# A mixture-of-experts layer on one core: three of four experts in seven products instead of two, casts and y tiles moved to ScalarE

## Chip, core and metric

The kernel runs on one core of a Trainium2 chip. The metric is the device time of one execution in microseconds, lower is better. Before the change the median of three runs is 317.22 us.

## What is computed

```python
x = x + tanh(g_xattn) * attention(layernorm(x), ctx)      # 2 x 1024 tokens of 256, 16 heads of 64, 64 context rows
h = layernorm(x)
probs = softmax(h.mean(axis=1) @ gate_w); top_w, top_i = top_k(probs, 2)     # per batch of 1024 tokens, 8 experts
for e in top_i:                                           # F = 1024
    hmid = gelu(h @ w1[e] + b1[e])
    out += top_w[e] * (hmid @ w2[e] + b2[e])
x = x + tanh(g_ffn) * out
```

Routing is per batch, so two batches need two experts each: four expert passes, numbered 0 to 3.

## The kernel before

**Precision.** Each float32 operand is a pair of float32r tiles: `_hi`, a rounded copy, and `_lo`, the remainder. A product is three matmuls (hi x hi, hi x lo, lo x hi). ScalarE makes most `_hi` tiles, VectorE the `_lo` tiles.

**Stages.** After the setup, a loop over 16 token tiles does attention in steps (scores, softmax, transposes of the probabilities from `sx`, products with `vw`). In it GpSimd multiplies the probabilities by the reciprocal sums (L563) and refines the layernorm factors by Newton steps (`y_rstds`, L529 to L535). The two last steps of the loop also start expert 0 (`EARLY`: hidden blocks 0, 1, 2). Then come the four expert passes, and the residual tiles are stored.

**Plain passes (experts 0 and 1 of the first batch).** For each of two chunks of 512 tokens and eight blocks f of 128 hidden columns, TensorE does `first_layer` (6 matmuls of 512 columns, into bank 4 or 5), ScalarE the Gelu into `gel`, VectorE `split(n)`: a cast to `h_hi` (L1318) and the subtraction to `h_lo` (L1320). TensorE does `second_layer` (6 matmuls) for the block two, in the first chunk four, behind. `first_layer(n)` from block 5 on waits for the Gelu of block n - 2, whose bank it takes. Along expert 0, eight y tiles of the second batch are made: GpSimd subtracts the mean and scales (L594, L597), TensorE transposes (L1658), ScalarE and VectorE make `yT_hi` and `yT_lo`. The next expert's weights are split in 32 pieces.

**Seven-product passes (experts 2 and 3 of the second batch).** A unit g handles blocks f and f + 4 for both chunks. Instead of eight block products of 3 matmuls it does seven, of sums and differences of weights (`wx`, from `block_sum`) and tokens (`t`, from `differences`). In between, TensorE does eight half second layers of the unit before (`behind_unit`, parts 0 to 7). ScalarE copies partial results out of the banks (`snapshot`, L855), VectorE adds (`block_total`, L1403), and four Gelus named C11, C22, C12, C21 read the sums. The order of unit 0 is P1, half, P2, half, P6, half, P5, P7, half, P3, P4; of the others half, P1, half, P2, half, P6, half, P5, half, P7, half, P3, half, P4, half (in unit 1 two halves precede P1). P7 waits for the second snapshot, P4 for the second total, P1 of the next unit for the Gelu C21.

**Order of work.** Each engine's program is written out by hand and runs in order; semaphores join them. A wait holds all that stands behind it on that engine. `FREE_SPLITS` is the constant 4 by which `w2_done` starts ahead, added by TensorE after the attention loop.

Of the kernel before, what the change touches and what calls it, by code (L numbers as in the profile page):

```python
# [5 lines left out]
def gated_cross_attention_moe_kernel(nc, x, xT, ctx_tokens, g_xattn, g_ffn, Wq, Wk, Wv, Wo, bo,  # L6
# [191 lines left out]
    with stack:  # L198
# [63 lines left out]
        def behind(q, c):  # L262

            return 4 if q == 0 and c == 0 else 2

        def staged(q):

            return 16 * (q // TOP + q % TOP)
# [3 lines left out]
        PIECES_ACT = [0, 0, 0, 0, 2, 1, 1, 1] + [0, 0, 0, 1] + [0, 0, 2, 2, 2, 2, 2, 0]
        PIECES_DVE = [0, 0, 0, 0, 0, 0, 0, 0] + [0, 1, 2, 2] + [0, 1, 1, 1, 2, 2, 2, 2]
        assert sum(PIECES_ACT) == sum(PIECES_DVE) == NCH * NF

        def place_of(c, f, between=False):

            return f if c == 0 and not between else f + NF - BETWEEN[0] if between else NF + len(BETWEEN) + f

        def pieces(table, q, c, f, between=False):  # L280


            if q > 0:
                return []
# [1707 lines left out]
```

## Time and profile before

| | us |
|---|---|
| median of three runs (lowest, highest) | 317.22 (317.11, 317.39) |
| the profiled execution, its own time | 317.35 |
| its span, first to last instruction | 315.6 |
| TensorE busy | 308.3 |
| VectorE busy | 261.8 |
| ScalarE busy | 178.6 |
| GpSimd busy | 84.5 |

The mean granted TensorE clock is 0.998 of full. In the profile, PE is TensorE, DVE is VectorE, ACT is ScalarE, POOL is GpSimd and SP the engine that issues most transfers. A matmul's duration overlaps that of the next, so the cadence of TensorE is read from starts, not from durations.

### The profile page before, as it was taken

The numbers are of one execution on the slowest core, as the hardware profiler recorded it, in microseconds if no ns is written. First come the engines' busy times: TensorE is split into PE (matmuls) and PEld (weight loads), VectorE is DVE, ScalarE is ACT, GpSimd is POOL, SyncE is SP. The second block draws the span as 40 slices with busy tenths as digits, with TensorE's granted clock in tenths as the row PEclk, the third lists the DMA queues.
The fourth block names the chain that finished last, engine by engine and source line by source line (L and its number), as shares of the span: only waits on it lengthen the run. The fifth ranks groups of instructions, "written<-read, shape, count | busy, mean of one in ns | idle before, by whom it ended". The sixth has DMA issues, their size and how long they took to land.

```text
span 315.6 us, 5546 instructions
## 1 busy us (share of the span) xinstructions
PE 308.3 (98%) x1837; PEld 265.3 (84%) x1837; DVE 261.8 (83%) x572; ACT 178.6 (57%) x571; POOL 84.5 (27%) x158
## 2 busy tenths in 40 slices
PE   8999999999999999999999999999999999999994
PEld 7978998788988999988788888888878887888884
DVE  1889999979889999999999589598899776875764
ACT  2648565686767667775466265273676553343430
POOL 1416547586466557344700000000000000000000
PEclk9999999999999999999999999999999999999999
DMA  7997200300000008700007070000000000010003
GB/s 270 386 337 10 34 3 1 133 3 1 2 0 3 0 2 275 258 3 0 0 2 267 8 260 0 1 2 0 0 1 2 0 0 2 0 66 36 34 0 135
DMA packets 21776, 20.02 MB, mean 63 GB/s; under 512 B 11692, under 2 KB 17268, under 8 KB 21364
## 3 DMA queue, kind: packets, MB, share of 16 engines
q1 hardware_dynamic: 21472, 19.14, 20.0%
q10 hardware_dynamic: 276, 0.52, 0.5%
q8 instruction: 15, 0.25, 0.3%
q14 instruction: 13, 0.11, 0.2%
HBM read 17.56 MB, written 2.11 MB: 62 GB/s over the span
## 4 chain that ended last, share of the span: by engine, by line
PE 72%; POOL 10%; issue 7%; DVE 6%; ACT 2%; DMA 2%; DVEq 0%; POOLq 0%
PE ps L1485 15%; PE ps L1486 15%; PE ps L1487 15%; PE ps L1829 4%; PE ps L1830 4%; PE ps L1831 4%; POOL sx L563 4%; PE ps L1505 2%; PE ps L1698 2%; PE ps L1699 2%; PE ps L1697 2%; POOL xs L583 2%; PE ps L1570 2%; POOL xs L581 2%; DMA wk_sb<-in_L_xattn_Wk_dram 2%
## 5 line engine op out<-in xcount | busy, mean ns | idle before, releaser
L695 ACT ACTIVATE sx<-ps,mx 128x64 f32<-128x64 f32 x128 | 38.3, 326 | 26.5 <-DVE mx L1071 26.4
L1320 DVE TENSOR_TENSOR h_lo<-gel,h_hi 128x512 fp32r<-128x512 f32 x64 | 44.9, 701 | 2.2
L563 POOL TENSOR_TENSOR sx<-sx,rs 128x512 f32<-128x512 f32 x32 | 33.5, 1066 | 41.5 <-DVE rs L1046 40.8
L839 ACT ACTIVATE gel<-ps,b1sel 128x512 f32<-128x512 f32 x32 | 21.8, 689 | 33.9 <-PE ps L1487 33.9
L1485 PE MATMUL ps<-h_hi,w_hi 128*128 128x512 f32 x96 | 38.0, 396 | 0.0
L1487 PE MATMUL ps<-h_hi,w_lo 128*128 128x512 f32 x96 | 37.5, 390 | 0.0
L1486 PE MATMUL ps<-h_lo,w_hi 128*128 128x512 f32 x96 | 37.4, 390 | 0.0
L1318 DVE CAST h_hi<-gel 128x512 fp32r<-128x512 f32 x64 | 28.2, 440 | 10.9 <-ACT gel L839 9.5
L1485 PE MATMUL ps<-vw,pT_hi 128*128 128x256 f32 x128 | 36.6, 286 | 0.1
L1487 PE MATMUL ps<-vw,pT_lo 128*128 128x256 f32 x128 | 36.2, 283 | 0.0
L1486 PE MATMUL ps<-vw,pT_hi 128*128 128x256 f32 x128 | 36.2, 283 | 0.0
L867 ACT ACTIVATE gel<-snap,b1sel 128x512 f32<-128x512 f32 x24 | 17.4, 724 | 25.4 <-DVE snap L1403 25.3
L1403 DVE TENSOR_TENSOR snap<-ps,snap 128x512 f32<-128x512 f32 x24 | 16.6, 690 | 18.0 <-PE ps L1831 17.8
L695 ACT ACTIVATION_READ_ACCUMULATOR sx<-ps,mx 128x1 f32 x128 | 27.9, 218 | 0.0
L1485 PE MATMUL ps<-a_hi,xT_hi 128*128 128x512 f32 x64 | 26.4, 413 | 0.1
L1485 PEld LDWEIGHTS ps<-vw,pT_hi 128*128 128x128 f32 x128 | 24.4, 191 | 2.0 <-issue 1.4
L1485 PE MATMUL ps<-yT_hi,w_hi 128*128 128x512 f32 x64 | 25.4, 396 | 0.0
L1487 PE MATMUL ps<-a_hi,xT_lo 128*128 128x512 f32 x64 | 25.1, 392 | 0.0
L1486 PE MATMUL ps<-a_lo,xT_hi 128*128 128x512 f32 x64 | 25.0, 390 | 0.0
L1487 PE MATMUL ps<-yT_hi,w_lo 128*128 128x512 f32 x64 | 24.9, 390 | 0.0
L1486 PE MATMUL ps<-yT_lo,w_hi 128*128 128x512 f32 x64 | 24.9, 390 | 0.0
L1486 PEld LDWEIGHTS ps<-vw,pT_hi 128*128 128x128 f32 x128 | 24.4, 191 | 0.4
(178 smaller groups left out, 804.2 us busy)
## 6 DMA issues: line engine op xcount, KB each, us to landing
stage_w<-in_L_ffn_w_dram SPq DMA_DIRECT2D x7, 1024.0 KB, 7.5
out_dram<-xt SPq DMA_DIRECT2D x7, 256.0 KB, 2.2
wqT<-in_L_xattn_Wq_dram SPq DMA_DIRECT2D x2, 512.0 KB, 7.1
wv_sb<-in_L_xattn_Wv_dram SPq DMA_DIRECT2D x2, 512.0 KB, 8.7
wo_sb<-in_L_xattn_Wo_dram SPq DMA_DIRECT2D x1, 1024.0 KB, 13.0
xt<-in_x_dram SPq DMA_DIRECT2D x1, 1024.0 KB, 9.8
xs<-in_xT_dram SPq DMA_DIRECT2D x1, 1024.0 KB, 11.0
spread<-x_stat SPq DMA_DIRECT2D x1, 1024.0 KB, 4.8
```

The source lines that it names most:

```text
L563: nc.gpsimd.tensor_tensor(pr, pr, rs[:, q, hs].unsqueeze(2).broadcast_to([P, H // 2, M]), ALU.mult).then_inc(mul_done, 1)
L695: last = nc.scalar.activation(sx[:, par, c0:c0 + M], ps[:, 2 * par + 1, c0 - BANK:c0 - BANK + M], ACT.Exp, bias=mx[:, par, h:h + 1], accum ...
L839: nc.scalar.activation(gel[:, f % 4, :], ps[:, h_bank, :], ACT.Gelu, bias=b1sel[:, 0, q, f:f + 1]).then_inc(gelu_done, 1)
L867: nc.scalar.activation(gel[:, n % 4, :], src, ACT.Gelu, bias=b1sel[:, 1, expert_of(g) % TOP, f:f + 1], scale=1.0 if i in (C11, C12) else - ...
L1318: nc.vector.tensor_copy(h_hi[:, n % 4, :], gel[:, n % 4, :]).then_inc(hhi_ready, 1)
L1320: nc.vector.tensor_tensor(h_lo[:, n % 4, :], gel[:, n % 4, :], as_f32(h_hi[:, n % 4, :]), ALU.subtract).then_inc(hlo_ready, 1)
L1403: nc.vector.tensor_tensor(snap[part][:, :], ps[:, bank, :], snap[part][:, :], ALU.add).then_inc(csum_done, 1)
L1485: mm(acc, hi_w, hi_x, start=start, stop=False)
L1486: mm(acc, hi_w, lo_x, start=False, stop=False)
L1487: return mm(acc, lo_w, hi_x, start=False, stop=stop)
L1829: mm(acc, w[0], y[0], start=start, stop=False, skip_group_check=True)
L1830: mm(acc, w[0], y[1], start=False, stop=False, skip_group_check=True)
```

## The change

Expert 1 goes through units as well: units 0 to 3 are expert 1, 4 to 7 expert 2, 8 to 11 expert 3 (`UNITS` = 4, `TURN` = 4, `FINAL` = 8). Only expert 0 stays plain. The token differences are made once per batch. The two accumulating banks are emptied (`finish(0, c)`) in unit 4, which gets an order of its own with one more half ahead of P1. Weights of experts 1 to 3 are split in whole blocks, `w2` in two parts of 1024 elements.

The cast to `h_hi` moves from VectorE to ScalarE for expert 0 and units 0 to 7 (`high(n)`); VectorE keeps the subtraction (`low(n)`). In units 8 to 11 VectorE does both. The y tiles of the second batch are made by ScalarE, one Identity activation with a scale and a bias per partition (`y_tile_1`), the first two behind the casts of blocks 0 and 1. The bias `shift2` = -mean * rstd is made by GpSimd for four tiles (two more operations at the end of the last Newton run) and by VectorE for four. ScalarE waits for the last attention output (`out_done`) ahead of its first cast.

```diff
             def y_rstds(i):
                 newton(*Y_PARTS[i], rstd2, ve_y, len(X_PARTS) + i + 1)
+                if Y_PARTS[i][0] == TB:
+                    tiles = slice(*Y_PARTS[i])
+                    link(nc.gpsimd.tensor_tensor(shift2[:, 0:TB // 2], mean2[:, tiles], rstd2[:, tiles], ALU.mult))
+                    link(nc.gpsimd.tensor_scalar(shift2[:, 0:TB // 2], shift2[:, 0:TB // 2], -1.0, None, ALU.mult))
                 pool.sem_inc(y_rstd, 1)
...
-            pool.wait_ge(sel_ready, 1)
-            for t in range(TB, NT):
-                if t == Y_PARTS[3][0]:
-                    pool.wait_ge(guess_ready, len(X_PARTS) + 4)
-                pool.wait_ge(yT_done, t - 1)
-                nc.gpsimd.tensor_tensor(yb[:, t % 2, :], xt[:, t, :], mean2[:, t:t + 1].broadcast_to([P, D]),
-                                        ALU.subtract).then_inc(xc_ready, 1)
-                pool.wait_ge(xc_ready, NT + t - TB)
-                nc.gpsimd.tensor_tensor(yb[:, t % 2, :], yb[:, t % 2, :], rstd2[:, t:t + 1].broadcast_to([P, D]),
-                                        ALU.mult).then_inc(y_ready, 1)
...
+            def y_tile_1(t):
+                if t < Y_PARTS[3][0]:
+                    act.wait_ge(y_rstd, 3)
+                else:
+                    act.wait_ge(guess_ready, len(X_PARTS) + 4)
+                act.wait_ge(yT_done, t - 1)
+                nc.scalar.activation(yb[:, t % 2, :], xt[:, t, :], ACT.Identity, scale=rstd2[:, t:t + 1],
+                                     bias=shift2[:, t - TB:t - TB + 1]).then_inc(y_ready, 1)
...
+            def high(n):
+                act.wait_ge(gelu_done, n + 1 + FREE_BANKS)
+                act.wait_ge(w2_done, n + 1)
+                nc.scalar.activation(h_hi[:, n % 4, :], gel[:, n % 4, :], ACT.Copy).then_inc(hhi_by_act, 1)
...
+            for n in range(N0):
+                act.wait_ge(h_done, n + 1)
+                act.wait_ge(hlo_ready, n + 1)
+                h_bank = EARLY_BANK[n] if n < 3 else 4 + n % 2
+                nc.scalar.activation(gel[:, n % 4, :], ps[:, h_bank, :], ACT.Gelu,
+                                     bias=b1sel[:, 0, 0, n % NF:n % NF + 1]).then_inc(gelu_done, 1)
                 if n == 0:
+                    act.wait_ge(out_done, NT)
+                high(n)
+                if n < 2:
+                    y_tile_1(TB + n)
+                along_expert_0(n)
...
                 gelu(g, C11)
                 snapshot(g, 1, ALPHA)
+                if by_act:
+                    high(h_of(g, C11))
                 snapshot(g, 2, DELTA)
...
                 gelu(g, C22)
+                if by_act:
+                    high(h_of(g, C22))
                 gelu(g, C12)
                 gelu(g, C21)
...
+            def low(n):
+                dve.wait_ge(hhi_by_act, n + 1)
+                nc.vector.tensor_tensor(h_lo[:, n % 4, :], gel[:, n % 4, :], as_f32(h_hi[:, n % 4, :]),
+                                        ALU.subtract).then_inc(hlo_ready, 1)
...
+                if n == 15:
+                    rows_low(1, 0)
+                    differences(1, 0)
+                    differences(1, 1)
...
                 block_total(g, 0)
                 if g == 0:
+                    differences_low(0, 3)
+                    rows_low(1, 1)
                     block_low(q + 1, 0)
...
+            def unit_at_turn(g):
+                behind_unit(g, 0)
+                behind_unit(g, 1)
+                product_1(g)
+                behind_unit(g, 2)
+                product_2(g)
...
```

**ScalarE at the start of expert 0.** The rows stand right behind the last attention copy; `gel` is a Gelu, `w_hi ... 128x1024` half of expert 0's second weights. Before:

```order
L632 ACTIVATE w_hi_109<-stage_w_0_106,swt 128x1024 [waits sel_ready,staged_w2_0]
L839 ACTIVATE gel<-ps,b1sel 128x512 [waits hlo_ready,h_done] x3
L632 ACTIVATE w_hi_109<-stage_w_0_106,swt 128x1024 [waits sel_ready,staged_w2_0]
L839 ACTIVATE gel<-ps,b1sel 128x512 [waits hlo_ready,h_done] x2
L762 ACTIVATE w_hi_131<-stage_w_1_129 128x128 [waits staged_w2_1,staged_w1_1,w2_done]
```

and now:

```order
L615 ACTIVATE w_hi_110<-stage_w_0_107,swt 128x1024 [waits sel_ready,staged_w2_0]
L812 ACTIVATE gel<-ps,b1sel 128x512 [waits hlo_ready,h_done]
L756 ACTIVATE h_hi<-gel 128x512 [waits w2_done,gelu_done,out_done]
L743 ACTIVATE yb<-xt,shift_56,rstd_57 128x256 [waits yT_done,y_rstd]
L812 ACTIVATE gel<-ps,b1sel 128x512 [waits hlo_ready,h_done]
L756 ACTIVATE h_hi<-gel 128x512 [waits w2_done,gelu_done]
L743 ACTIVATE yb<-xt,shift_56,rstd_57 128x256 [waits yT_done,y_rstd]
L812 ACTIVATE gel<-ps,b1sel 128x512 [waits hlo_ready,h_done]
L756 ACTIVATE h_hi<-gel 128x512 [waits w2_done,gelu_done]
L615 ACTIVATE w_hi_110<-stage_w_0_107,swt 128x1024 [waits sel_ready,staged_w2_0]
L812 ACTIVATE gel<-ps,b1sel 128x512 [waits hlo_ready,h_done]
```

Ahead of the fourth Gelu, the one of block 3, there now stand three casts and two y tiles as well, and the first cast waits for `out_done`.

**VectorE from the last block ahead of the first unit to that unit's totals.** `snap` rows are `block_total`. Before, where expert 1's last block is followed by the first unit of expert 2:

```order
L1318 CAST h_hi<-gel 128x512 [waits w2_done,gelu_done]
L1320 TENSOR_TENSOR h_lo<-gel,h_hi 128x512 [waits hhi_ready]
L1272 SCALAR_TENSOR_TENSOR w_lo_110<-stage_w_0_106,swt,w_hi_109 128x256 [waits w2x_hi_done] x2
L1403 TENSOR_TENSOR snap_115<-ps,snap_115 128x512 [waits snap_done,prod_done]
L1265 TENSOR_TENSOR wx_lo_142<-stage_w_1_129,wx_hi_133 128x512 [waits wx_hi_done] x2
L1318 CAST h_hi<-gel 128x512 [waits w2_done,gelu_done]
L1320 TENSOR_TENSOR h_lo<-gel,h_hi 128x512 [waits hhi_ready]
L1403 TENSOR_TENSOR snap_143<-ps,snap_143 128x512 [waits snap_done,prod_done]
L1381 TENSOR_SCALAR oT<-ps,b2sel 128x512 [waits w2_done]
L1403 TENSOR_TENSOR snap_134<-ps,snap_134 128x512 [waits snap_done,prod_done]
```

and now, where expert 0's last block is followed by the first unit of expert 1:

```order
L1286 TENSOR_TENSOR h_lo<-gel,h_hi 128x512 [waits hhi_by_act]
L1241 SCALAR_TENSOR_TENSOR w_lo_137<-stage_w_1_131,swt,w_hi_136 128x1024 [waits w2x_hi_done]
L1250 TENSOR_TENSOR traw_140<-yT_hi,yT_lo 128x512 [waits ylo_ready]
L1250 TENSOR_TENSOR traw_140<-yT_hi,yT_lo 128x512
L1398 TENSOR_TENSOR snap_116<-ps,snap_116 128x512 [waits snap_done,prod_done]
L1281 TENSOR_TENSOR t_lo<-traw_139,t_hi 128x512 [waits t_hi_done]
L1241 SCALAR_TENSOR_TENSOR w_lo_137<-stage_w_1_131,swt,w_hi_136 128x1024 [waits w2x_hi_done]
L1234 TENSOR_TENSOR wx_lo_132<-stage_w_0_106,wx_hi_115 128x512 [waits w2x_lo_done,wx_lo_done,wx_hi_done]
L1286 TENSOR_TENSOR h_lo<-gel,h_hi 128x512 [waits hhi_by_act]
L1398 TENSOR_TENSOR snap_133<-ps,snap_133 128x512 [waits snap_done,prod_done]
L1398 TENSOR_TENSOR snap_135<-ps,snap_135 128x512 [waits snap_done,prod_done]
```

Between the last block's `h_lo` and the first total there now stand a 1024-element subtraction and two sums for the second batch, and between the first and the second total another 1024-element one and a `t_lo`, with one `wx_lo` and no cast.

**GpSimd at the last Newton run** (`nu_p`, `rstd`), ahead of the multiplications of the probabilities `sx` of tile 14, now:

```order
L524 TENSOR_TENSOR nu_p<-nu_p,rstd_57 128x4 [waits pool_step]
L525 TENSOR_SCALAR nu_p<-nu_p 128x4 [waits pool_step]
L526 TENSOR_TENSOR rstd_57<-nu_p,rstd_57 128x4 [waits pool_step]
L533 TENSOR_TENSOR shift_56<-mean_55,rstd_57 128x4 [waits pool_step]
L534 TENSOR_SCALAR shift_56<-shift_56 128x4 [waits pool_step]
L558 TENSOR_TENSOR sx<-sx,rs 128x512 [waits pool_step,recip_done]
L558 TENSOR_TENSOR sx<-sx,rs 128x512
```

The two `shift` rows are new; before, the `sx` row followed the `rstd` row.

## Rows read from the trace of the kernel before

**Rows 1.** The page, part 1: busy us (share of the span) and instructions.

```profile
PE 308.3 (98%) x1837; PEld 265.3 (84%) x1837; DVE 261.8 (83%) x572; ACT 178.6 (57%) x571; POOL 84.5 (27%) x158
```

**Rows 2.** Timeline, TensorE, start of expert 0: start, us, engine, line, operation.

```profile
138.16 0.40 PE L1485 MATMUL ps<-yT_hi,w_hi 128*128 128x512 f32 x1
...
142.26 0.39 PE L1485 MATMUL ps<-yT_hi,w_hi 128*128 128x512 f32 x1
...
152.32 0.39 PE L1487 MATMUL ps<-h_hi,w_lo 128*128 128x512 f32 x1
152.67 0.44 PE L1658 MATMUL ps<-ident,yb 128*128 128x128 f32 x2
```

**Rows 3.** Timeline, ScalarE, start of expert 0.

```profile
134.32 1.15 ACT L632 ACTIVATE w_hi<-stage_w,swt 128x1024 fp32r<-128x1024 f32 x1
135.36 1.85 ACT L839 ACTIVATE gel<-ps,b1sel 128x512 f32<-128x512 f32 x3
139.74 0.69 ACT L839 ACTIVATE gel<-ps,b1sel 128x512 f32<-128x512 f32 x1 [1.50 <-PE ps L1487]
```

**Rows 4.** Groups by form, ScalarE, 133 to 312 us: busy us, mean ns.

```profile
L776 ACT ACTIVATE wx_hi<-stage_w 128x512 fp32r<-128x512 f32 x14 | 8.3, 626 | 2.3 <-DVE stage_w L1258 2.2
L784 ACT ACTIVATE w_hi<-stage_w,swt 128x256 fp32r<-128x256 f32 x16 | 7.5, 500 | 0.0
L765 ACT ACTIVATE w_hi<-stage_w,swt 128x128 fp32r<-128x128 f32 x16 | 6.3, 395 | 0.0
...
L762 ACT ACTIVATE w_hi<-stage_w 128x128 fp32r<-128x128 f32 x16 | 4.8, 303 | 0.0
```

**Rows 5.** Timeline, GpSimd and TensorE, tiles 14 and 15 of attention.

```profile
123.61 0.22 POOL L534 TENSOR_SCALAR nu_p<-nu_p 128x4 f32<-128x4 f32 x1
123.92 0.20 POOL L535 TENSOR_TENSOR rstd<-nu_p,rstd 128x4 f32<-128x4 f32 x1
124.30 1.04 POOL L563 TENSOR_TENSOR sx<-sx,rs 128x512 f32<-128x512 f32 x1 [0.18 <-POOL rstd L535]
...
126.06 1.04 PE L1570 MATMUL ps<-ident,sx 128*128 128x128 f32 x8
...
134.74 0.39 PE L1487 MATMUL ps<-yT_hi,w_lo 128*128 128x512 f32 x1
135.21 0.36 PE L1485 MATMUL ps<-vw,pT_hi 128*128 128x256 f32 x1
```

**Rows 6.** Timeline, TensorE and ScalarE, the first two units.

```profile
229.93 0.28 PE L1699 MATMUL ps<-w_hi,h_lo 128*128 128x256 f32 x1
230.21 0.50 PE L1829 MATMUL ps<-yT_hi,wx_hi 128*128 128x512 f32 x1
...
234.90 0.39 PE L1487 MATMUL ps<-h_hi,w_lo 128*128 128x512 f32 x1
235.29 0.50 PE L1829 MATMUL ps<-t_hi,wx_hi 128*128 128x512 f32 x1
...
234.03 0.72 ACT L867 ACTIVATE gel<-snap,b1sel 128x512 f32<-128x512 f32 x1 [1.42 <-DVE snap L1403]
234.66 1.06 ACT L855 ACTIVATE snap<-ps 128x512 f32<-128x512 f32 x2
```

**Rows 7.** Groups by form (133 to 312 us) and timeline, VectorE.

```profile
L1320 DVE TENSOR_TENSOR h_lo<-gel,h_hi 128x512 fp32r<-128x512 f32 x64 | 44.9, 701 | 2.2
L1318 DVE CAST h_hi<-gel 128x512 fp32r<-128x512 f32 x64 | 28.2, 440 | 10.9 <-ACT gel L839 9.5 <-ACT gel L867 1.2 <-DVE rstd L943 0.2
L1403 DVE TENSOR_TENSOR snap<-ps,snap 128x512 f32<-128x512 f32 x24 | 16.6, 690 | 18.0 <-PE ps L1831 17.8
...
147.72 1.30 DVE L1202 SCALAR_TENSOR_TENSOR w_lo<-stage_w,swt,w_hi 128x1024 fp32r<-128x1024 f32 x1
148.95 0.83 DVE L1318 CAST h_hi<-gel 128x512 fp32r<-128x512 f32 x1
```

**Rows 8.** Windows view, one unit: PE, PEld, DVE, ACT, POOL busy us, then PEclk.

```profile
243.00:253.00 10.00, 10.00 (x57) 8.75 (x56) 7.82 (x15) 6.11 (x11) 0.00 (x0) 1.00 0.00 0
```

More of the change, by code:

```diff
@@ L260, in gated_cross_attention_moe_kernel, with behind @@
         OWN_BANK = 5
[L262 to L268, printed above, removed]
+        def behind(c):
+            return 4 if c == 0 else 2
         BETWEEN = range(4, NF)
[L272 to L284, printed above, removed]
-            n = place_of(c, f, between)
-            return [(i // NF, i % NF) for i in range(sum(table[:n]), sum(table[:n + 1]))]
         UNITS = NF // 2
-        LAST = TOP * UNITS - 1
-        N0 = TOP * NCH * NF
+        LAST = (NQ - 1) * UNITS - 1
+        N0 = NCH * NF
+        TURN, FINAL = UNITS, 2 * UNITS
         ALPHA, BETA, DELTA, SPARE = 4, 5, 6, 7
@@ L353, in sum_is_through @@
             if b == 0:
-                eng.wait_ge(w2_done, FREE_SPLITS + ((TOP - 1) * NCH + c + 1) * NF)
+                eng.wait_ge(w2_done, FREE_SPLITS + h_of(TURN - 1, (C21, C12)[c]) + 1)
             else:
@@ L830, in _ @@
[L830 to L850 removed]
+                if n == 8:
+                    rows_high(1, 0)
@@ new lines, in unit @@
+                if g == FINAL:
+                    b2_row()
+                block_total(g, 2)
+                remainder(g, C22)
+                if g == 0:
+                    block_low(q + 1, 1)
+                    differences(1, 2)
+                if g == 1:
+                    block_sum(q + 1, 2)
+                    block_sum(q + 1, 3)
+                    differences(1, 4)
+                if g == 2:
+                    block_low(q + 1, RAW + 2)
+                    differences(1, 6)
+                    differences(1, 7)
@@ L1739, in half_of @@
                 if g % UNITS == 0 and i == C11 and d == 0:
-                    pe.wait_ge(w2x_lo_done, counted(q, NF, NF))
-                if g == 0 and i == C11 and d == 0:
-                    pe.wait_ge(oT0_ready, NCH)
-                    pe.wait_ge(oT1_ready, NCH)
+                    pe.wait_ge(w2x_lo_done, counted(q, 2, 2))
+                if g == TURN and i in (C11, C22) and d == 0:
+                    pe.wait_ge(oT0_ready, (C11, C22).index(i) + 1)
+                    pe.wait_ge(oT1_ready, (C11, C22).index(i) + 1)
+                if q < TOP:
+                    second_layer_half(c, f, n, d, w2_hi[slot], w2_lo[slot], False, (g, i) == (TURN - 1, (C21, C12)[c]))
+                    return
                 if c == 0:
```

624 lines of the change are left out of this document (314 added, 310 removed).

## Prediction

> **What bounds the kernel now.** The page comes first: TensorE is busy 308.3 of 315.6 us, VectorE 83%, ScalarE 57%, GpSimd 27% [rows 1]. Busy TensorE time counts overlapped ends, so the second view is the timeline of TensorE by starts. From 138.16 to 142.26 us stand 18 matmuls of 512 columns, 4.10 us, a cadence of 0.228 us with nothing between [rows 2]. From there to the tail TensorE hardly ever waits: a first layer, a second layer or a product of three matmuls follows at once. So the expert passes are worth what their matmuls are worth, and any wait that the change makes on TensorE is paid in full. The reader is to see in the rows below which instruction TensorE would wait for, and what stands ahead of that instruction on its own engine. The sum is made against the profiled execution, 317.35 us, which is 0.13 above the median of the runs.
>
> **Matmuls removed.** A plain pair of hidden blocks takes 8 block products for both chunks, a unit 7, of 3 matmuls each. Four units save 12 matmuls: 12 x 0.228 = 2.73 us gained. Second layers, transposes and routing keep their number.
>
> **Stalls that the old first units had.** Unit 0's last token-tile matmul starts at 229.93 and P1 of unit 1 at 230.21, 0.16 above the 0.12 between such matmuls, and that first matmul holds the next for another 0.10 (0.50 long instead of 0.40). P7 of unit 1 starts 0.39 after its forerunner, 0.16 too late, with 0.11 behind it; the Gelu at 234.03 and the snapshot behind it, at 234.66, released it [rows 6]. Together 0.53 us. Those waits came with the switch from a plain pass into units. That switch now stands between experts 0 and 1 and is counted by itself below, so here the 0.53 goes.
>
> **GpSimd ahead of tile 14.** Its last Newton run gets two operations more. Their spacing is 0.31 for a scalar one, [rows 5] 123.61 to 123.92, and 0.28 for the other kind: 0.59 us. The `sx` multiplication followed at 124.30, with 0.18 idle that is put down to that Newton run, so it is late by the whole 0.59. Its two halves (1.04 for the first) then end near 125.93 and 126.93; TensorE's second four transposes, due near 126.50 (126.06 plus four of the eight), start 0.46 late. At 134.74 to 135.21 TensorE waited 0.24 above its cadence for VectorE's part of tile 15, which had work of its own ahead of it; that wait is swallowed. Net cost 0.22 us. Bounds: 0 if the reciprocal were the releaser, 0.59 if nothing is swallowed.
>
> **ScalarE at the start of expert 0.** This is the largest term. TensorE's first layer of block 5 (142.26) waits for the Gelu of block 3, since they share bank 5. Before, that Gelu ran at 139.74, 2 us early [rows 3]. Now ScalarE makes the first Gelu near 136 and then stands at the cast of block 0, which needs the last attention output: the matmul in front of 138.16 [rows 2] is the last of these, ending near 138.35. Queued behind that wait are two Gelus, two casts, two y tiles, the second half of `w2_hi` and the Gelu of block 3. Prices: a cast like `wx_hi`, 0.626 long, with the next start 0.52 after it (successive activations overlap by 0.10: three Gelus took 1.85, so 0.58 each against 0.69 alone). A Gelu that its own cast waits for: 0.69 + 0.04. The half `w2_hi`: 1.04 to the next start. A y tile isn't in the trace: 256 columns with one operand per partition take 0.500, and one such operand costs 0.395 - 0.303 = 0.092 [rows 4], so with two 0.59, spacing 0.49 (bounds 0.40 and 0.59, the 256-column copy's spacing and a whole Gelu's). From 138.35: cast 138.87, y tile 139.36, Gelu 140.09, cast 140.61, y tile 141.10, Gelu 141.83, cast 142.35, `w2_hi` 143.39, Gelu of block 3 to 144.08, and 0.04 to release. TensorE starts block 5 at 144.12 instead of 142.26: 1.86 us lost. The whole chain rests on ScalarE; bounds 1.6 and 2.2.
>
> After it ScalarE is behind by less than a slot of 2.7 us per block, and the casts of blocks 4 to 7 wait for second layers (`w2_done`) that TensorE has by then issued. Walking the same prices on, the Gelu of block 9 ends about 1 us ahead of the first layer that needs its bank, so I count nothing more. At 152.32 to 152.67 TensorE waited 0.12 above cadence for a y tile's remainder on VectorE [rows 2]; with TensorE 1.9 us later that goes.
>
> A rule of the Trainium skill bears on this. In the stretch where GpSimd made y tiles a cast on VectorE took 0.83 instead of the mean 0.44 [rows 7]. The page "GPSIMD Engine Reference", section 1, Specifications, says that GpSimd's SBUF interfaces are shared with VectorE, with contention for two-port or two-input instructions. By it the move gives VectorE its speed back; by the rows TensorE waited for VectorE there only 0.12 us, so either way the sum is the same.
>
> Another speaks against the change: "ScalarE: Activation LUTs", Rules for kernel authors, sends adds and multiplies to VectorE. The rows agree in price, 0.440 for the cast on VectorE and 0.626 on ScalarE. By that rule the casts of blocks 0 to 2 would have stayed, and the 1.86 would not arise.
>
> **The new first unit.** It follows expert 0's last block. Take 0 as the start of its P1; a slot of three matmuls is 0.68, so P2 is at 1.36, P6 at 2.72, P5 at 4.08, P7 at 4.76, P3 at 6.12, P4 at 6.80, P1 of the next unit at 8.84. A product can be read 0.91 after its start. VectorE: block 15's `h_lo` starts at 0.25 (its Gelu and cast end at 0.22) and takes 0.61 to the next start. Then the 1024-element subtraction: one took 1.30 and the next started 1.23 later [rows 7]; I take 1.2. Two sums at 0.60: the first total starts at 3.25, ends at 3.94. Before, it could start as soon as P2 was through. The Gelu C11 starts at 3.97, the second snapshot 0.63 later with 0.60, as in [rows 6], so P7 starts at 5.25 instead of 4.76 and its first matmul drags 0.1. VectorE goes on: `t_lo` 0.6, the second 1024-element subtraction 1.3 (the next waits for its end), `wx_lo` 0.6, `h_lo` 0.6: the second total starts at 6.96 and ends at 7.65. P4 starts at 7.70, 0.90 late. Then Gelu C22 7.68 to 8.40, its cast, Gelu C12 at 8.96, Gelu C21 9.60 to 10.29, so P1 of unit 1 starts at 10.33 instead of 8.84; with its slow first matmul 1.60 us lost. Bounds: 0.5 (if VectorE gets through 1.1 us sooner) and 2.0.
>
> **The other units.** A unit gives TensorE 10.2 us. ScalarE gets four casts, 4 x 0.52 = 2.1 us more than the 6.11 per 10 us of a unit with weight copies [rows 8], some 8.2; VectorE loses four casts, 4 x 0.45. The tight place is the Gelu C22, cast, Gelu C12, Gelu C21, then P1: before, ScalarE idled about 0.6 between C22 and C12, which is what the cast takes, and C21 ended about 0.5 ahead of P1. I count 0. In unit 4 the second snapshot, the emptying of the banks and the first half of unit 5 each have 0.3 us or more to spare by the same walk.
>
> **Sum.** 317.35 - 2.73 - 0.53 - 0.12 + 0.22 + 1.86 + 1.60 = 317.65; 0.13 less for the median: 317.5 us. What the matmuls give, two places of waiting take back.
>
> **Rivals.** First, **the stall at the units is not there**: VectorE reaches both totals in time because its order leaves it more lead than my walk gives, and TensorE loses only at the start of expert 0. For it: VectorE idles at several places in the passes (18.0 us ahead of the totals, [rows 7]). Against it: the two 1024-element subtractions stand just there. Time 317.5 - 1.6 = 315.9; if the start stall is halved as well, 315.0. Chance 0.27.
>
> Second, **ScalarE becomes the bound in the units**: the cast between C22 and C12 pushes C21 past P1. It decides when the pair of cast and wait takes more than the 0.6 + 0.5 us of room; each of the seven units 1 to 7 would then lose some 0.2 to 0.4, together 2.1, giving 319.6. For it: the load of 8.2 of 10.2 with waits inside. Against: the room, which is a full cast and more. Chance 0.20.
>
> Third, **the change doesn't do what it says**, the early stall being hidden because TensorE has other work: its program has none between block 4's second-layer part and block 5. Chance 0.05, 315.7.
>
> **How the numbers follow.** The forecast has 0.48, with its own range 316.8 to 318.2 from the bounds. About 0.6 us (0.2%) is what a measurement of this kernel can tell from no change: below 316.6 is faster, above 317.8 slower. Faster: the first and third rivals less a part that ends near 316.6, 0.30. Slower: the second, and of the forecast's 0.48 about 0.13 above 317.8, 0.33. Same: 0.37. Leaving out 0.1 at either end the range is 315.2 to 319.0.
>
> **What would show each step.** TensorE's first layer of block 5 starts some 6 us behind that of block 3 instead of 4.1, with a wait put down to ScalarE's `gel`. GpSimd's `sx` row for tile 14 lies 0.6 us later against the Newton run's start. P7 and P4 of unit 0 and P1 of unit 1 show waits for `snap` and `gel`, together 1.5 us. Units 2 to 7 are 10.2 to 10.4 us long with no waits. Wrong would be: no wait at block 5, or a wait at the end of every unit.

## The result and the profile after

The changed kernel takes 318.27 us (median of 7 runs, 317.70 to 318.50), the kernel before 317.22 (7 runs); the ratio of the two is 1.0025, 95% interval 1.0015 to 1.0035. Measured once more (experiment 5) it was 317.88 against 317.29, ratio 1.0021 (1.0011 to 1.0031). So it is slower, by 0.6 to 1.1 us (0.2 to 0.3%). The profiled execution took 318.28 us with a span of 316.5; TensorE's mean granted clock was 1.000 of full, against 0.998 before.

The page, part 1, of the kernel after, to be read beside [rows 1]:

```profile
PE 306.1 (97%) x1825; PEld 263.6 (83%) x1825; DVE 255.2 (81%) x518; ACT 213.0 (67%) x608; POOL 72.4 (23%) x144
```

The 12 matmuls are gone (1837 to 1825) and TensorE's busy time is 2.2 us less, but the span is 0.9 longer: TensorE waits more. ScalarE has 34 us more to do, VectorE 7 and GpSimd 12 less. Three places hold the waits.

**GpSimd ahead of tile 14.** Timeline of GpSimd and TensorE (start, us, engine, line; in brackets the idle time and who ended it), beside [rows 5]:

```profile
124.50 0.20 POOL L533 TENSOR_TENSOR shift<-mean,rstd 128x4 f32<-128x4 f32 x1
124.79 0.23 POOL L534 TENSOR_SCALAR shift<-shift 128x4 f32<-128x4 f32 x1
125.20 2.49 POOL L558 TENSOR_TENSOR sx<-sx,rs 128x512 f32<-128x512 f32 x2 [0.18 <-POOL shift L534]
...
126.39 0.60 PE L1595 MATMUL ps<-ident,sx 128*128 128x128 f32 x4
127.75 0.66 PE L1595 MATMUL ps<-ident,sx 128*128 128x128 f32 x4 [0.76 <-POOL sx L558]
```

The multiplication starts 0.98 us behind the last `rstd` row (at 124.22), where it started 0.38 behind it before: 0.60 us later, as forecast (0.59). But it takes 2.49 us for its two halves, where it took 2.04 before. TensorE's second four transposes come 1.36 us behind the first four.

**ScalarE at the start of expert 0**, beside [rows 2] and [rows 3]:

```profile
139.20 0.63 ACT L756 ACTIVATE h_hi<-gel 128x512 fp32r<-128x512 f32 x1 [2.01 <-PE ps L1512]
139.74 0.59 ACT L743 ACTIVATE yb<-xt,shift,rstd 128x256 f32<-128x256 f32 x1
140.23 0.67 ACT L812 ACTIVATE gel<-ps,b1sel 128x512 f32<-128x512 f32 x1
140.93 0.63 ACT L756 ACTIVATE h_hi<-gel 128x512 fp32r<-128x512 f32 x1
...
143.19 1.13 ACT L615 ACTIVATE w_hi<-stage_w,swt 128x1024 fp32r<-128x1024 f32 x1
144.23 0.67 ACT L812 ACTIVATE gel<-ps,b1sel 128x512 f32<-128x512 f32 x1
...
139.00 0.40 PE L1510 MATMUL ps<-yT_hi,w_hi 128*128 128x512 f32 x1
...
144.95 0.50 PE L1510 MATMUL ps<-yT_hi,w_hi 128*128 128x512 f32 x1 [1.69 <-ACT gel L812]
```

The cast of block 0 (`h_hi<-gel`) waits 2.01 us for the last attention output. Behind it the queue is the forecast one, step for step. Block 3 starts at 139.00, block 5 at 144.95: 5.95 us instead of 4.10.

**The new first unit.** P1 of unit 0 is at 180.28; P7, P4 and P1 of unit 1 stand here, and VectorE's queue ahead of the two totals (`snap<-ps,snap`), beside [rows 6]:

```profile
185.50 0.50 PE L1850 MATMUL ps<-t_hi,wx_hi 128*128 128x512 f32 x1 [0.30 <-ACT snap L831]
188.09 0.50 PE L1850 MATMUL ps<-t_hi,wx_hi 128*128 128x512 f32 x1 [0.24 <-DVE snap L1398]
190.69 0.50 PE L1850 MATMUL ps<-yT_hi,wx_hi 128*128 128x512 f32 x1 [0.28 <-ACT gel L843]
...
180.51 0.69 DVE L1286 TENSOR_TENSOR h_lo<-gel,h_hi 128x512 fp32r<-128x512 f32 x1 [0.23 <-ACT h_hi L756]
181.12 1.28 DVE L1241 SCALAR_TENSOR_TENSOR w_lo<-stage_w,swt,w_hi 128x1024 fp32r<-128x1024 f32 x1
182.32 1.29 DVE L1250 TENSOR_TENSOR traw<-yT_hi,yT_lo 128x512 f32<-128x512 f32 x2
183.52 0.68 DVE L1398 TENSOR_TENSOR snap<-ps,snap 128x512 f32<-128x512 f32 x1
...
184.72 1.28 DVE L1241 SCALAR_TENSOR_TENSOR w_lo<-stage_w,swt,w_hi 128x1024 fp32r<-128x1024 f32 x1
...
187.35 1.28 DVE L1398 TENSOR_TENSOR snap<-ps,snap 128x512 f32<-128x512 f32 x2
```

All three matmuls wait, and the waits are put down to the snapshot, the total and the Gelu that the walk named. P1 of unit 1 comes 10.41 us behind P1 of unit 0 (forecast 10.33).

From there to unit 7 TensorE doesn't wait once. The windows view of unit 2 (columns as in [rows 8]) has VectorE busy for 8.5 and ScalarE for 8.7 of 10.2 us, ScalarE 0.5 more than the forecast's 8.2:

```profile
200.36:210.56 10.20, 10.20 (x46) 8.45 (x45) 8.47 (x14) 8.72 (x16) 0.00 (x0) 1.00 0.00 0
```

### The profile page after: what moved, and what is told of

It is laid out like the page before. It is cut to its first block, busy times and chain, and to the rows that moved or that the text cites. A ratio compares the mean times of both kernels' runs of the same rounds, so it can differ in the third digit from the quotient of the medians.

```text
span 316.5 us, 5518 instructions
## 1 busy us (share of the span) xinstructions
PE 306.1 (97%) x1825; PEld 263.6 (83%) x1825; DVE 255.2 (81%) x518; ACT 213.0 (67%) x608; POOL 72.4 (23%) x144
## 4 chain that ended last, share of the span: by engine, by line
PE 63%; POOL 12%; DVE 10%; issue 9%; ACT 4%; DMA 1%; DVEq 0%; ACTq 0%; POOLq 0%
PE ps L1510 10%; PE ps L1512 10%; PE ps L1511 10%; PE ps L1850 6%; PE ps L1851 6%; PE ps L1852 6%; POOL sx L558 4%; PE ps L1530 2%; PE ps L1721 2%; PE ps L1722 2%; PE ps L1720 2%; DVE mx L1071 2%; POOL xs L578 2%; POOL xs L576 2%; ACT sx L678 1%
## 5 line engine op out<-in xcount | busy, mean ns | idle before, releaser
L843 ACT ACTIVATE gel<-snap,b1sel 128x512 f32<-128x512 f32 x36 | 26.1, 724 | 28.8 <-DVE snap L1398 28.8
L1398 DVE TENSOR_TENSOR snap<-ps,snap 128x512 f32<-128x512 f32 x36 | 24.8, 690 | 21.8 <-PE ps L1852 21.4
L1286 DVE TENSOR_TENSOR h_lo<-gel,h_hi 128x512 fp32r<-128x512 f32 x48 | 32.4, 688 | 9.0 <-ACT h_hi L756 8.2
L756 ACT ACTIVATE h_hi<-gel 128x512 fp32r<-128x512 f32 x48 | 29.3, 627 | 5.1 <-PE ps L1512 4.5
L831 ACT ACTIVATE snap<-ps 128x512 f32<-128x512 f32 x36 | 21.5, 596 | 11.1 <-PE ps L1852 11.0
L1030 DVE TENSOR_TENSOR pT_lo<-ps,pT_hi 128x512 fp32r<-128x512 f32 x32 | 20.6, 684 | 5.0 <-ACT pT_hi L690 4.6
L1512 PEld LDWEIGHTS ps<-vw,pT_lo 128*128 128x128 f32 x128 | 24.4, 191 | 0.0
L1512 PEld LDWEIGHTS ps<-h_hi,w_lo 128*128 128x128 f32 x96 | 18.0, 188 | 3.9
```

What stands on the lines that cost most here:

```text
L756: nc.scalar.activation(h_hi[:, n % 4, :], gel[:, n % 4, :], ACT.Copy).then_inc(hhi_by_act, 1)
L831: nc.scalar.activation(snap[k][:, :], ps[:, bank, :], ACT.Copy).then_inc(snap_done, 1)
L843: nc.scalar.activation(gel[:, n % 4, :], src, ACT.Gelu, bias=b1sel[:, batch_of(g), expert_of(g) % TOP, f:f + 1], scale=1.0 if i in (C11, C ...
L1030: nc.vector.tensor_tensor(pT_lo[:, par, 4 * half:4 * half + 4, :], ps[:, 4 + half, :].rearrange("p (m i) -> p m i", m=4), as_f32(pT_hi[:, ...
L1286: nc.vector.tensor_tensor(h_lo[:, n % 4, :], gel[:, n % 4, :], as_f32(h_hi[:, n % 4, :]), ALU.subtract).then_inc(hlo_ready, 1)
L1398: nc.vector.tensor_tensor(snap[part][:, :], ps[:, bank, :], snap[part][:, :], ALU.add).then_inc(csum_done, 1)
```

## The experiments

Times of single profiles shift as a whole, by up to 0.8 us, from the first loads on (experiment 5), so traces are compared from the first `sx` multiplication of GpSimd on: TensorE's last matmul comes 286.27 us behind it in the kernel before and 287.02 in the kernel after, 0.75 us later. That figure is called **the distance** below. Each kernel has one profile and 4 to 10 timed executions; ratios and intervals are those of the times.

| kernel | median us | beside before | ratio to before (95%) | distance |
|---|---|---|---|---|
| 1: cast of block 0 on VectorE | 316.09 | 317.25 | 0.9959 (0.9942 to 0.9976) | 285.28 |
| 2: `shift2` later | 317.58 | 317.25 | 1.0005 (0.9987 to 1.0023) | 286.45 |
| 3: VectorE's order spread | 317.03 | 317.25 | 0.9984 (0.9960 to 1.0008) | 286.05 |
| 4: all three | 314.50 | 317.25 | 0.9908 (0.9880 to 0.9937) | 283.40 |
| 5: after, again | 317.88 | 317.29 | 1.0021 (1.0011 to 1.0031) | 287.11 |
| 6: before + two operations | 317.81 | 317.29 | 1.0017 (1.0007 to 1.0026) | 286.58 |
| 7: y tiles on GpSimd | 316.45 | 317.29 | 0.9977 (0.9967 to 0.9987) | 285.54 |
| 8: units' casts on VectorE | 319.96 | 317.29 | 1.0082 (1.0065 to 1.0099) | 287.99 |
| 9: 4 + Gelus in a row | 315.32 | 317.40 | 0.9933 (0.9920 to 0.9947) | 284.22 |
| 10: differences late | 316.96 | 317.40 | 0.9988 (0.9979 to 0.9997) | 286.01 |
| 11: 9 + VectorE swapped | 314.16 | 317.33 | 0.9916 (0.9894 to 0.9937) | 283.11 |
| 12: 4 again | 314.52 | 317.33 | 0.9911 (0.9898 to 0.9923) | 283.44 |

### Experiment 1: the cast of block 0

```diff
-                if n == 0:
-                    act.wait_ge(out_done, NT)
-                high(n)
+                if n >= EARLY_CASTS:
+                    if n == EARLY_CASTS:
+                        act.wait_ge(out_done, NT)
+                    high(n)
...
             for n in range(N0):
-                low(n)
+                (split if n < EARLY_CASTS else low)(n)
```

with `EARLY_CASTS` 1; the first part is ScalarE's loop, the second VectorE's.

> The cast of block 0 alone goes back to VectorE; ScalarE keeps every other cast and all y tiles. Theory A, the queue behind the wait: in the profile of the kernel after, ScalarE stood 2.01 us at the cast of block 0 until the last attention output, with two y tiles and two Gelus behind it. Without that cast its first y tile starts near 137.1 and the Gelu of block 1 before 139; the cast of block 1 starts at 139.2, then y tile 0.49, Gelu 0.70, cast 0.53, w2_hi 1.04, Gelu of block 3 to about 143.2, against a first layer of block 5 due at 143.1. The wait there falls from 1.84 us to about 0.1 and the time by 1.75: 316.5 us. Rival B, too much work on ScalarE: only the one cast of 0.5 us is gained, 317.8 us.

316.09 us; the distance is 1.74 less than after's. ScalarE and the first layer of block 5:

```profile
136.66 0.61 ACT L744 ACTIVATE yb<-xt,shift,rstd 128x256 f32<-128x256 f32 x1
...
138.79 0.63 ACT L757 ACTIVATE h_hi<-gel 128x512 fp32r<-128x512 f32 x1 [0.94 <-PE ps L1514]
...
142.10 0.67 ACT L813 ACTIVATE gel<-ps,b1sel 128x512 f32<-128x512 f32 x1
...
142.47 0.39 PE L1514 MATMUL ps<-h_hi,w_lo 128*128 128x512 f32 x1
142.82 0.50 PE L1512 MATMUL ps<-yT_hi,w_hi 128*128 128x512 f32 x1
```

The first y tile and the Gelu of block 1 now run ahead of the wait, and the wait at block 5 is 0.13 us (its forerunner is at 142.47, 0.36 earlier instead of 0.23). One cast of 0.54 us moved, 1.74 gained: it was the place of the cast in ScalarE's queue, not its length. Theory A holds.

### Experiment 2: `shift2` later

```diff
                 newton(*Y_PARTS[i], rstd2, ve_y, len(X_PARTS) + i + 1)
-                if Y_PARTS[i][0] == TB:
-                    tiles = slice(*Y_PARTS[i])
-                    link(nc.gpsimd.tensor_tensor(shift2[:, 0:TB // 2], mean2[:, tiles], rstd2[:, tiles], ALU.mult))
-                    link(nc.gpsimd.tensor_scalar(shift2[:, 0:TB // 2], shift2[:, 0:TB // 2], -1.0, None, ALU.mult))
-                pool.sem_inc(y_rstd, 1)
+                if Y_PARTS[i][0] < TB:
+                    pool.sem_inc(y_rstd, 1)
...
+                if s == 16:
+                    y_shifts()
```

`y_shifts` holds the two operations and the third increment of `y_rstd`, behind the multiplication of tile 15.

> The two GpSimd operations that make shift2 are moved from ahead of the multiplication of tile 14 to behind that of tile 15. Theory A, the displaced multiplication: in the kernel after, it started 0.59 us later and took 2.49 instead of 2.04 us, and the first layer of block 3 came 0.56 us later than the 0.29 by which everything was late. Moved away, the multiplication takes 2.04 us again and the time falls by 0.55: 317.7 us. Rival B, the size that the prediction gave: 0.22 us, so 318.05. Rival C: shift2 now comes too late for the first y tile on ScalarE and nothing is gained.

317.58 us, distance 0.57 to 0.66 less than after's two. The multiplication takes 2.05 us again:

```profile
124.09 2.05 POOL L562 TENSOR_TENSOR sx<-sx,rs 128x512 f32<-128x512 f32 x2
...
132.53 0.20 POOL L537 TENSOR_TENSOR shift<-mean,rstd 128x4 f32<-128x4 f32 x1
...
134.57 0.40 PE L1518 MATMUL ps<-yT_hi,w_lo 128*128 128x512 f32 x1
135.12 0.36 PE L1516 MATMUL ps<-vw,pT_hi 128*128 128x256 f32 x1 [0.15 <-DVE pT_lo L1036]
```

The transposes of tile 14 no longer wait (0.9 us gained), but the wait for VectorE's part of tile 15 is back, 0.32 above the cadence, and that is the wait that the prediction called swallowed. Net 0.6, theory A. The first y tile was not late.

### Experiments 3 and 10: VectorE's order

```diff
                 if n == 9:
+                    rows_low(1, 0)
                     block_sum(1, 2)
...
-                if n == 15:
-                    rows_low(1, 0)
-                    differences(1, 0)
-                    differences(1, 1)
```

The eight steps `differences(1, 0)` to `(1, 7)` keep their order and move to units 0 (one), 1 (three) and 2 (four). Experiment 10 moves them alone; there `if n == 15:` and `rows_low(1, 0)` stay.

> VectorE's order alone is changed: the 1024-element subtraction rows_low(1, 0) goes from block 15 to block 9, and the eight steps of the second batch's differences start behind total 2 of unit 0 instead of at block 15. Theory A, VectorE's queue ahead of the first total: the total starts about 1 us earlier, right behind P2; P7 and P4 of unit 0 don't wait, and P1 of unit 1 waits about 0.3 us for the fourth Gelu (Gelu, cast, Gelu, Gelu behind total 1). 1.3 us gained: 317.0 us. Rival B: units 1 to 3 then wait for VectorE, which has more to do there, and 0.5 us or less is gained. Rival C, ScalarE is what is late in the first unit (casts between its Gelus): the three waits stay as they are, 318.2 us.

> The kernel after with only the differences moved (the eight steps start behind total 2 of unit 0); rows_low(1, 0), the 1024-element subtraction, stays at block 15, ahead of the first total. Theory A, only the last 1.2 us of VectorE's queue make the first total late, since it can't start before P2 is through, 1.2 us earlier than it did: the same 1.0 to 1.1 us gained as by moving both, 317.0 us. Rival B, each of the two pieces counts for half: 317.5 us.

317.03 and 316.96 us, distances 0.97 and 1.01 less than after's: the same. Experiment 10's VectorE and P1 of unit 1:

```profile
180.75 1.28 DVE L1241 SCALAR_TENSOR_TENSOR w_lo<-stage_w,swt,w_hi 128x1024 fp32r<-128x1024 f32 x1
182.15 0.69 DVE L1396 TENSOR_TENSOR snap<-ps,snap 128x512 f32<-128x512 f32 x1
...
189.33 0.50 PE L1853 MATMUL ps<-yT_hi,wx_hi 128*128 128x512 f32 x1 [0.26 <-ACT gel L843]
```

The first total starts right behind the 1024-element subtraction, 2.24 us after P1 of unit 0 (at 179.91). In experiment 3, where VectorE stood idle for P2 instead, it was 2.24 us too. So only the last 1.2 us of VectorE's queue counted, as theory A of experiment 10 says. P7 and P4 start at most 0.01 us late, though P4's first matmul still holds the next for 0.11; 0.43 us of waiting for the fourth Gelu stays at P1 of unit 1, 0.1 more than I had expected. Units 1 to 3 took the moved work without a wait.

### Experiments 4 and 12: all three

> The casts of blocks 0 to 2 on VectorE, shift2 behind the multiplication of tile 15, and VectorE's order spread as above, all three together. Theory A, the three waits are independent and each is paid in full on TensorE: 1.95 + 0.55 + 1.3 = 3.8 us less than the kernel after, 314.5 us, and faster than the kernel before by 2.7 (the matmuls removed). Rival B, behind each wait stands another one: the gains don't add up, 315.5 us or more.

> The fourth experiment again, unchanged, for the comparison on the same chip with the run before it: 314.5 us.

Here the casts of blocks 0, 1 and 2 are on VectorE, not that of block 0 alone as in experiment 1. 314.50 and 314.52 us, as expected. The three gains one by one are 1.74, 0.57 and 0.97 us of distance, 3.3 together; all at once they are 3.6. The 0.2 that experiment 1 had left at block 5 (0.13 of waiting and 0.11 of the slow matmul behind it) is gone here too. So the gains add up, and no other wait stood behind these. It is faster than the kernel before by 0.9%. The prediction's own sum has 3.38 us for the matmuls and old waits (2.73 + 0.53 + 0.12). Left in the first unit are 0.54 at P1 of unit 1 and 0.12 at P4; 3.38 - 0.66 is 2.72, and the distance is 2.87 less than before's.

### Experiment 5: the kernel after again

> The kernel after, unchanged, again. It lost 0.29 us ahead of 98 us, where the change touches nothing; in the first four experiments the start of the same stretch lay up to 0.4 us apart. Theory A, the 0.29 is variation of the first load (the context landed 0.24 us later than in the profile of before): the stretch ahead of 98 us is back within 0.1 us of before's in this profile, or elsewhere again, and the median stays between 317.9 and 318.3. Rival B, it belongs to the kernel (its own code): 0.29 again, 318.3 us.

The first `sx` multiplication in the profiles of before, after and this run:

```profile
24.89 2.05 POOL L563 TENSOR_TENSOR sx<-sx,rs 128x512 f32<-128x512 f32 x2 [6.91 <-DVE rs L1046]
25.18 2.05 POOL L558 TENSOR_TENSOR sx<-sx,rs 128x512 f32<-128x512 f32 x2 [6.90 <-DVE rs L1046]
24.34 2.05 POOL L558 TENSOR_TENSOR sx<-sx,rs 128x512 f32<-128x512 f32 x2 [6.92 <-DVE rs L1046]
```

The same program starts 0.84 us apart; rival B falls. The distance is 287.11, within 0.1 of the first profile. The 0.29 us was never the kernel's. (The median, 317.88, came just under the stretch that I gave.)

### Experiment 6: the kernel before with the two operations

```diff
                 newton(*Y_PARTS[i], rstd2, ve_y, len(X_PARTS) + i + 1)
+                if Y_PARTS[i][0] == TB:
+                    tiles = slice(*Y_PARTS[i])
+                    link(nc.gpsimd.tensor_tensor(shift2[:, 0:TB // 2], mean2[:, tiles], rstd2[:, tiles], ALU.mult))
+                    link(nc.gpsimd.tensor_scalar(shift2[:, 0:TB // 2], shift2[:, 0:TB // 2], -1.0, None, ALU.mult))
                 pool.sem_inc(y_rstd, 1)
```

> The kernel before with nothing added but the two GpSimd operations that make shift2, at the place where the change has them; nothing reads their result. It measures the GpSimd term of the prediction alone. Theory A: the multiplication of tile 14 starts 0.59 us later and, meeting VectorE's work, takes 2.49 instead of 2.04 us; TensorE waits 0.9 us at the transposes of tile 14 and the 0.24 us at tile 15 go: 0.55 us more than the kernel before, 317.8 us. Rival B, the prediction's size: the multiplication stays at 2.04 us, 0.22 us more, 317.45 us.

317.81 against 317.29 us:

```profile
124.88 2.49 POOL L568 TENSOR_TENSOR sx<-sx,rs 128x512 f32<-128x512 f32 x2 [0.18 <-POOL shift L544]
...
126.10 0.60 PE L1575 MATMUL ps<-ident,sx 128*128 128x128 f32 x4
127.43 0.66 PE L1575 MATMUL ps<-ident,sx 128*128 128x128 f32 x4 [0.74 <-POOL sx L568]
```

The multiplication takes 2.49 us here too, in a kernel that has nothing else of the change. Behind the transposes of tile 14 the kernel is 0.77 us behind the kernel before; 0.30 comes back at tile 15 and 0.17 at the y tile that [rows 2] shows waiting, so the distance is 0.31 more. Theory A's mechanism holds; its 0.55 leaves out the y tile. The medians lie 0.52 apart, and their interval (0.07 to 0.26%, 0.2 to 0.8 us) holds both figures.

Which work of VectorE it meets is in the same traces. It is the subtraction `w_lo` (two inputs, both in SBUF). GpSimd's second half and that subtraction in the kernel before, and the subtraction here:

```profile
125.30 1.04 POOL L563 TENSOR_TENSOR sx<-sx,rs 128x512 f32<-128x512 f32 x1
...
125.61 1.28 DVE L1188 TENSOR_TENSOR w_lo<-stage_w,w_hi 128x512 fp32r<-128x512 f32 x1
...
125.60 0.88 DVE L1193 TENSOR_TENSOR w_lo<-stage_w,w_hi 128x512 fp32r<-128x512 f32 x1
```

Before, GpSimd's second half had begun when the subtraction began; the half took 1.04 us and the subtraction 1.28. Here the subtraction begins at the same time, 125.60, but 0.29 us ahead of the second half (125.89), and the half takes 1.49 and the subtraction 0.88. All 14 profiles fall into these two groups (the subtraction 1.18 to 1.28 beside 1.04, or 0.87 to 0.90 beside 1.49): whichever of the two began later is the long one. At tile 15 of the kernel before a `w_lo` of the same form began first (130.09) and took 0.63 us, and GpSimd's half behind it, at 130.25, took 1.36. (The 0.88 us here is longer than that 0.63; this subtraction began behind GpSimd's first half.) No run moved the subtraction alone, so this is read from the traces and not tested.

### Experiment 7: y tiles on GpSimd again

The GpSimd loop of y tiles comes back as in the kernel before, `y_tile_1`, its calls and `shift2` go.

> The kernel after with its second part undone: the y tiles on GpSimd again, shift2 gone; the seven-product units and all casts on ScalarE stay. Theory A: the two operations on GpSimd go (0.55 us gained) and ScalarE's queue ahead of the Gelu of block 3 is shorter by two y tiles of 0.49 (0.98 us gained, the wait at block 5 falls from 1.84 to 0.86); VectorE slowed by GpSimd costs 0.1 again. 318.2 - 1.4 = 316.8 us. Rival B: VectorE, slowed while GpSimd makes tiles (0.83 for a cast in the kernel before), makes h_lo late, so that half of that is lost: 317.5 us or more.

316.45 us, distance 1.5 less than after's:

```profile
138.04 0.63 ACT L752 ACTIVATE h_hi<-gel 128x512 fp32r<-128x512 f32 x1 [2.31 <-PE ps L1503]
138.58 0.67 ACT L808 ACTIVATE gel<-ps,b1sel 128x512 f32<-128x512 f32 x1
...
142.82 0.50 PE L1501 MATMUL ps<-yT_hi,w_hi 128*128 128x512 f32 x1 [0.71 <-ACT gel L808]
...
L1277 DVE TENSOR_TENSOR h_lo<-gel,h_hi 128x512 fp32r<-128x512 f32 x16 | 12.5, 783 | 1.8 <-ACT h_hi L752 1.5
L1286 DVE TENSOR_TENSOR h_lo<-gel,h_hi 128x512 fp32r<-128x512 f32 x15 | 10.3, 686 | 2.6 <-ACT h_hi L756 2.5
```

The wait at block 5 is 0.87 us (1.10 from its forerunner), half of what it was: two y tiles fewer behind the cast. VectorE does pay: `h_lo` takes 0.783 us on average from 133 to 180 us, against 0.686 without GpSimd's tiles. But no TensorE wait follows from it. So the y tiles on ScalarE, with `shift2`, cost 1.5 us as they stand, and the rest, the units with all moved casts on ScalarE, is 0.7 to 0.8 us faster than the kernel before (0.73 in distance, 0.84 in medians).

The page "GPSIMD Engine Reference" of the Trainium skill, section 1, Specifications, says that VectorE and GpSimd share SBUF interfaces and contend on them. By that rule, the trace agrees, in both directions: `h_lo` at 0.783, and the multiplication of tile 14 at 2.49.

### Experiment 8: the units' casts on VectorE

```diff
+        CAST_UNITS = 0
...
-                q, by_act = expert_of(g), g < FINAL
+                q, by_act = expert_of(g), g < CAST_UNITS
...
-                if g < FINAL:
+                if g < CAST_UNITS:
                     low(h_of(g, i))
                 else:
                     split(h_of(g, i))
```

> The kernel after with the 32 casts of units 0 to 7 on VectorE, as units 8 to 11 have them; those of expert 0 stay on ScalarE. Theory A, VectorE is short of time in units 0 to 3, where it idled 0.8 us (unit 1) and 1.6 us (unit 2) and gets 4 x 0.45 us more in each: the first unit stays about as it is (the cast between its Gelus is gone, 0.5 us, but VectorE is later by as much), unit 1 and 2 lose about 1 us together: 319.2 us. Rival B, ScalarE's casts are what make P1 of unit 1 late: 0.5 us gained and nothing lost, 317.7 us.

319.96 us, slower than either expectation. P4 of unit 0 and P7 of unit 2:

```profile
188.31 0.50 PE L1851 MATMUL ps<-t_hi,wx_hi 128*128 128x512 f32 x1 [0.69 <-DVE snap L1399]
...
206.30 0.50 PE L1851 MATMUL ps<-t_hi,wx_hi 128*128 128x512 f32 x1
```

In unit 0 the wait at P4 grew from 0.41 to 0.86 us and the one at P1 of unit 1 went, a draw as theory A has it. Units 1 and 2 lost about 0.8 together, where theory A had 1. That is the distance, 0.9 more. Another 1.0 us lies behind TensorE's last matmul: from there to the end of the span it is 5.3 us, and 4.3 in both profiles of the kernel after. 0.83 of it is in the issue of the last two stores:

```profile
312.97 0.96 SPq L492 DMA_DIRECT2D out_dram<-xt  x2
313.69 1.79 SPq L493 DMA_DIRECT2D out_dram<-xt  x2
```

Their issue on SyncE took 1.79 us instead of 0.96. No other profile here has it (0.95 to 0.97), and the times of this kernel's runs agree with it (319.85 to 320.04; the median is 2.1 us above experiment 5's, on the same chip); nothing was tried that explains it, and it stays open. For the change it says: ScalarE was the right engine for the casts inside the units.

### Experiments 9 and 11: the last Gelus of unit 0

```diff
                 gelu(g, C22)
-                if by_act:
+                if by_act and g > 0:
                     high(h_of(g, C22))
                 gelu(g, C12)
                 gelu(g, C21)
+                if g == 0:
+                    high(h_of(g, C22))
...
                 block_total(g, 2)
+                if g == 0:
+                    block_low(q + 1, 1)
+                    differences(1, 0)
                 remainder(g, C22)
```

Both on top of experiment 4. The first part is ScalarE's and in both, the second VectorE's and in experiment 11 alone.

> The fourth experiment (casts of blocks 0 to 2 on VectorE, shift2 late, VectorE's order spread) with one thing more: in unit 0 ScalarE makes its last three Gelus in a row and the cast of C22 behind them. What TensorE still waited there was 0.42 us at P1 of unit 1 and 0.10 in its first matmul. Theory A, that wait is the cast in front of the two last Gelus: C21 ends 0.54 us earlier, the wait goes, 314.5 - 0.5 = 314.0 us. Rival B: TensorE then waits the same time for h_lo of C22 behind P1, since its cast is late; 314.5 us.

> As the ninth experiment (the three Gelus in a row), but VectorE does wx_lo and the first step of the differences ahead of h_lo of C22 in unit 0. There the wait at P1 of unit 1 was gone, 0.5 us, and yet the kernel lost 0.8 against the fourth: VectorE stood 1.88 us at h_lo of C22, whose cast came after the three Gelus, and was late at unit 1's first total. Theory A, that standing is the whole loss: the 1.2 us of work that need no cast now fill it, the first total of unit 1 comes 1.2 us earlier, and both gains remain: 314.1 us. Rival B, any later h_lo of C22 is paid in unit 1 (VectorE has 0.8 us of idle time there): 314.5 us or more.

Experiment 9: 315.32 us, 0.8 slower than experiment 4. The wait at P1 of unit 1 fell to 0.08 us, and P7 of unit 1 got one of 0.55 and P1 of unit 2 one of 0.21. P7:

```profile
187.17 0.69 DVE L1296 TENSOR_TENSOR h_lo<-gel,h_hi 128x512 fp32r<-128x512 f32 x1 [1.88 <-ACT h_hi L763]
...
192.16 0.50 PE L1862 MATMUL ps<-t_hi,wx_hi 128*128 128x512 f32 x1 [0.39 <-ACT snap L839]
```

Neither expectation had it: not TensorE but VectorE stood for the late cast, 1.88 us at `h_lo` of C22, and its queue was late for the rest of unit 1. Experiment 11 puts 1.2 us of other work in front:

```profile
185.30 0.69 DVE L1260 TENSOR_TENSOR traw<-yT_hi,yT_lo 128x512 f32<-128x512 f32 x1
186.67 1.90 DVE L1296 TENSOR_TENSOR h_lo<-gel,h_hi 128x512 fp32r<-128x512 f32 x3 [0.68 <-ACT h_hi L763]
...
186.17 0.50 PE L1862 MATMUL ps<-yT_hi,wx_hi 128*128 128x512 f32 x1
```

VectorE stands 0.68 us, TensorE 0.08, and the kernel takes 314.16 us (314.52 for experiment 4 on the same chip; 0.3 less in distance). Its median is the lowest of all, though one of its six executions took 316.35, and it is faster than the kernel before by some 0.8% (ratio 0.9894 to 0.9937). From experiment 4 the intervals don't tell it apart. Its distance is 0.3 less, where two profiles of one program lay within 0.1 (experiments 4 and 12, the kernel after and experiment 5), and the rows show the wait gone.

## Why the prediction was right, and where its sizes were not

The forecast was 317.5 us in a range of 315.2 to 319.0, by gains on TensorE that two waits take back. The time was 318.27, and 317.88 when measured again. In distance the sum forecast 0.30 us more than before, and it was 0.75. The first of these times lies 0.07 above the forecast's own range (316.8 to 318.2), the second inside it. Both lie above 317.8, where the prediction has "slower" begin: it had given that 0.33, and 0.37 to no change it could tell.

- **Matmuls and old stalls**: 2.73 + 0.53 + 0.12. Experiment 4, where the new waits are mostly gone, has 2.87 us less distance and 0.66 left in the first unit; 3.38 - 0.66 is 2.72. Held, within 0.15.
- **ScalarE at the start of expert 0**: 1.86 forecast, 1.85 measured, and every link of the chain within 0.03 us (the y tile 0.59 long and 0.49 to the next start, the interpolated price). The first matmul behind the wait then held the next by 0.11, which the sum counted at other waits and forgot here: 1.95. Experiment 1 shows the mechanism: it is the wait in front of the queue. Rival three falls: the wait was there.
- **The new first unit**: 1.60 forecast; P7 0.56, P4 0.51 and P1 of unit 1 0.54 above the cadence with their slow first matmuls, 1.61. Experiment 10 shows that VectorE's queue made the first two of them, and experiments 9 and 11 that the third was the cast between ScalarE's Gelus. Rival one falls.
- **The other units**: 0 forecast, 0 measured, though ScalarE was busy 8.7 us in unit 2 and not 8.2. Rival two falls, and by experiment 8 the opposite choice is the one that would have cost.
- **GpSimd ahead of tile 14** is the term that failed, in size. The step "its two halves then end near 125.93 and 126.93" moved the multiplication by 0.59 us and kept its length. Its second half came behind a `w_lo` subtraction of VectorE instead of ahead of it and took 0.45 more, so TensorE lost 0.85 at the transposes instead of 0.46. Tile 15 gave 0.30 back instead of 0.24. Net 0.54 instead of 0.22, near the far bound of 0.59. Experiment 6 shows the same 2.49 us with the two operations alone, and its rows the subtraction. The trace of the kernel before had the sign of it: the same multiplication took 2.41 us at tile 15.

Together: 0.32 for GpSimd and 0.09 for the slow first matmul make 0.41 of the 0.45 us between forecast and measurement. The profiled execution has 0.29 more from its first loads, which is no part of the change (experiment 5). The chance of 0.33 for slower had this outcome in it by the forecast's upper part. The cause is the one given there, waits at the two named places, with the GpSimd term as the third. The two errors of size have the same sign, so neither hid the other.

A rule of the Trainium skill bears on the largest term: "ScalarE: Activation LUTs", Rules for kernel authors, sends adds and multiplies to VectorE. It doesn't name casts. Taken for them too, the trace agrees for the casts of blocks 0 to 2 (experiment 4, 1.95 us) and disagrees for those of the units (experiment 8, 0.9 us lost where VectorE was the shorter of time): what decided was whose queue had room there, and in what order. The y tiles are a multiplication and an addition, and no run put them on VectorE.

## What to carry to other kernels

Before a wait is put on an in-order engine, list what is queued behind it: a cast of 0.54 us cost 1.74 because it stood for an attention output in front of work that was ready (experiment 1), and the same happened on VectorE when its cast came late (experiment 9). Where work is moved between engines, the gain on TensorE is kept only if the totals at the seam stay on time; putting 1.2 us of work that nobody needs yet behind the seam gave 1.0 us (experiment 10). An operation that slides in time can take another length than the one it had: look at what the other engine does in its new place. Here the same multiplication stood in the trace of before with 2.04 and with 2.41 us, and got 2.49.
